# Projections of x and ctx as fp32 products instead of three fp32r passes of split operands

## What is computed

```python
# x: (32, 64, 256), ctx: (32, 64, 128), pos: (32, 64, 2), all fp32
def xattn(x, ctx, pos, Wq, Wkv, Wout, bout):        # 32 heads of 8
    q = (x @ Wq).reshape(b, n, 32, 8)
    k, v = split(ctx @ Wkv, 2)                       # each (b, n, 32, 8)
    q, k = rope(q, pos), rope(k, pos)
    w = softmax(einsum('bqhd,bkhd->bhqk', q, k) / sqrt(8))
    return einsum('bhqk,bkhd->bqhd', w, v).reshape(b, n, 256) @ Wout + bout

x = x + xattn(layernorm(x), ctx, pos, ...)
x = x + soft_moe(layernorm(x), ...)                  # 16 experts of 128 slots, untouched here
```

## Time and profile before

| | |
|---|---|
| device time, median of three runs | 481.79 us (481.67 to 482.77) |
| the profiled execution | 482.33 us, span 480.4 us |
| TensorE busy (matmul) | 445.4 us, 93% of the span |
| VectorE busy | 389.0 us, 81% |
| ScalarE busy | 286.8 us, 60% |
| GpSimd busy | 182.6 us, 38% |
| mean granted TensorE clock | 0.979 of full |

### The profile page before, as it was taken

The page is one execution under the profiler, slowest core; times in us unless marked ns, Lnnn a source line. Parts: engine busy times, 40 slices in busy tenths (PEclk is TensorE's granted clock), DMA queues, the critical chain, the costliest instruction groups (busy, mean ns, idle before and its releaser), DMA issues.

```text
span 480.4 us, 12796 instructions
## 1 busy us (share of the span) xinstructions
PE 445.4 (93%) x4816; PEld 383.2 (80%) x4816; DVE 389.0 (81%) x857; ACT 286.8 (60%) x553; POOL 182.6 (38%) x322
## 2 busy tenths in 40 slices
PE   0679899999999989899999999999999999999995
PEld 0557788778887767778889988988988988988994
DVE  5689788898889985977977977977977887797793
ACT  3357677777888775264465466456457457456532
POOL 4489988469996332114112112112112212202100
PEclk9879799999999999899999999999999999999999
DMA  8930000000002000123223223312312312322321
GB/s 234 279 134 24 2 3 23 1 4 1 1 3 71 3 2 1 41 55 93 57 55 90 57 59 82 75 49 72 82 49 66 93 50 55 98 51 53 94 63 49
DMA packets 27815, 28.54 MB, mean 59 GB/s; under 512 B 10960, under 2 KB 19072, under 8 KB 27520
## 3 DMA queue, kind: packets, MB, share of 16 engines
q1 hardware_dynamic: 27776, 28.00, 22.4%
HBM read 9.11 MB, written 2.10 MB: 23 GB/s over the span
## 4 chain that ended last, share of the span: by engine, by line
PE 68%; DVE 17%; SPq 5%; POOL 4%; DMA 3%; issue 2%; ACT 2%; DVEq 0%; ACTq 0%; POOLq 0%
PE bank L996 12%; PE bank L998 11%; PE bank L997 11%; PE bank L1212 9%; PE bank L1092 6%; PE bank L1230 5%; SPq L293 4%; PE bank L1056 3%; PE bank L1075 3%; PE bank L1113 2%; DVE kT L748 2%; DVE pT L894 2%; DMA xa<-in_x 2%; DVE pb L758 2%; DVE mx L753 2%
## 5 line engine op out<-in xcount | busy, mean ns | idle before, releaser
L894 DVE STREAM_TRANSPOSE pT<-eb 128x512 f32<-128x512 f32 x64 | 44.7, 701 | 37.6 <-ACT eb L618 34.6
L1212 PE MATMUL bank<-w_raw,eb 128*128 128x130 f32 x512 | 62.5, 281 | 0.6 <-DVE w_raw L885 0.6
L1212 PEld LDWEIGHTS bank<-w_raw,eb 128*128 128x128 f32 x512 | 60.2, 195 | 1.9 <-DVE w_raw L885 1.6
L629 ACT ACTIVATE pb<-pb 128x768 f32<-128x768 f32 (+1 forms) x48 | 37.2, 774 | 33.4 <-DVE pb L920 33.4
L624 ACT CAST xlT_h<-bank 128x256 fp32r<-128x256 f32 x16 | 5.9, 371 | 77.6 <-PE bank L1184 77.6
L996 PE MATMUL bank<-mun_h,xlT_l 128*128 128x512 f32 x128 | 52.1, 407 | 0.0
L920 DVE TENSOR_TENSOR pb<-bank,rh 128x384 f32<-128x384 f32 x96 | 49.3, 513 | 3.3
L618 ACT ACTIVATE eb<-bank,nshift,rn 128x512 f32<-128x512 f32 x64 | 46.2, 776 | 7.7 <-PE bank L998 7.6
L998 PE MATMUL bank<-mun_h,xlT_h 128*128 128x512 f32 x128 | 50.5, 395 | 0.0
L997 PE MATMUL bank<-mun_l,xlT_h 128*128 128x512 f32 x128 | 50.5, 394 | 0.0
L545 ACT COPY pT<-bank 128x512 f32<-128x512 f32 x64 | 37.6, 588 | 20.6 <-PE bank L1075 19.7
(11 more groups left out here) (159 smaller groups left out, 1157.1 us busy)
## 6 DMA issues: line engine op xcount, KB each, us to landing
mu_raw<-pT SPq DMA_DIRECT2D x256, 64.0 KB, 2.0
mu_raw<-in_L_ffn_mu SPq DMA_DIRECT2D x1, 2048.0 KB, 10.5
out<-w_raw SPq DMA_DIRECT2D x16, 128.0 KB, 1.9
xa<-in_x SPq DMA_DIRECT2D x1, 1536.0 KB, 8.4
w_raw<-in_L_ffn_W SPq DMA_DIRECT2D x2, 512.0 KB, 9.9
w_raw<-in_L_ffn_W SPq DMA_DIRECT2D x1, 1024.0 KB, 7.8
xa<-in_x SPq DMA_DIRECT2D x1, 512.0 KB, 3.5
ctile<-in_ctx SPq DMA_DIRECT2D x1, 512.0 KB, 5.2
```

The costliest lines, as they stand in the source:

```text
L894: v.transpose(eblk[:, :, 4 * c:4 * c + 4, :].rearrange("p m e j -> p e m j"), eb[:, 4 * c:4 * c + 4, :].rearrange("p e (m j) -> p e m j", ...
L1212: m = mm(bank[HB[i]][:, n * 2 * HC:(n + 1) * 2 * HC], eb[:, e, :], xw[:, e, :], start=True, stop=True)
```

## The change

The split of x, ctx and their weights goes. `wqkv` and `xT` become single fp32 tiles; the weights are loaded straight into their place; ScalarE copies the transposes once, as fp32; each product is one fp32 matmul call. The wait that kept bank 7 in order for `mu_clamp` is now written at `mu_clamp` itself, on ScalarE's copy. The rest of the kernel, and the order of work on every engine, stay.

```diff
-        wqkv = split("wqkv", P, KD + 2, DIM)
+        wqkv = sb("wqkv", P, KD + 2, DIM)
-        xT = split("xT", P, 2, 3, P)
+        xT = sb("xT", P, 2, 3, P)
...
-            sp.dma_start(wqkv_raw[:, 0:KD, :], Wq.rearrange("(k p) n -> p k n", p=P)).then_inc(wqkv_loaded, 16)
-            sp.dma_start(wqkv_raw[:, KD:KD + 2, :], Wkv.rearrange("p (k n) -> p k n", k=2)).then_inc(wqkv_loaded, 16)
+            sp.dma_start(wqkv[:, 0:KD, :], Wq.rearrange("(k p) n -> p k n", p=P)).then_inc(wqkv_loaded, 16)
+            sp.dma_start(wqkv[:, KD:KD + 2, :], Wkv.rearrange("p (k n) -> p k n", k=2)).then_inc(wqkv_loaded, 16)
...
-            act.wait_ge(wqkv_loaded, 32)
-            a.copy(flat(wqkv[0]), flat(wqkv_raw)).then_inc(wqkv_step, 1)
...
-            def xT_high(t):
+            def xT_copy(t):
                 act.wait_ge(xT_filled, t + 1)
-                a.copy(flat(xT[0][:, t % 2]), bank[7][:, 0:3 * P]).then_inc(xT_split, 1)
+                a.copy(flat(xT[:, t % 2]), bank[7][:, 0:3 * P]).then_inc(xT_ready, 1)
...
-            def xT_low(t):
-                dve.wait_ge(xT_split, t + 1)
-                v.tensor_tensor(flat(xT[1][:, t % 2]), bank[7][:, 0:3 * P], flat(xT[0][:, t % 2]).bitcast(F32), ALU.subtract)\
-                    .then_inc(xT_ready, 1)
...
             def mu_clamp(q):
                 dve.wait_ge(muss_ready, q + 1)
+                dve.wait_ge(xT_ready, q + 6)
...
-                if s + 2 < TILES:
-                    xT_low(s + 2)
...
-            dve.wait_ge(wqkv_step, 1)
-            v.tensor_tensor(flat(wqkv[1]), flat(wqkv_raw), flat(wqkv[0]).bitcast(F32), ALU.subtract)\
-                .then_inc(wqkv_ready, 1)
-            xT_low(0)
...
                 for k in range(KD):
-                    mm3(bank[4][:, 0:DIM], [h[:, t % 2, k, :] for h in xT], [h[:, k, :] for h in wqkv],
-                        first=(k == 0), last=(k == KD - 1))
-                mm3(bank[4][:, DIM:2 * DIM], [h[:, t % 2, KD, :] for h in xT], [h[:, KD, :] for h in wqkv])\
+                    mm(bank[4][:, 0:DIM], xT[:, t % 2, k, :], wqkv[:, k, :], start=(k == 0), stop=(k == KD - 1))
+                mm(bank[4][:, DIM:2 * DIM], xT[:, t % 2, KD, :], wqkv[:, KD, :], start=True, stop=True)\
                     .then_inc(qk_filled, 1)
...
-                mm3(bank[6][:, 0:DIM], [h[:, t % 2, KD, :] for h in xT], [h[:, KD + 1, :] for h in wqkv])\
+                mm(bank[6][:, 0:DIM], xT[:, t % 2, KD, :], wqkv[:, KD + 1, :], start=True, stop=True)\
                     .then_inc(v_filled, 1)
...
-            pe.wait_ge(wqkv_ready, 1)
+            pe.wait_ge(wqkv_loaded, 32)
             project_qk(0)
```

More of the change, by code:

```diff
@@ L154, in build @@
         mu_ready = sem("mu_ready")
-        wqkv_step = sem("wqkv_step")
-        wqkv_ready = sem("wqkv_ready")
         shift_step = sem("shift_step")
@@ L166, in build @@
         xT_filled = sem("xT_filled")
-        xT_split = sem("xT_split")
         xT_ready = sem("xT_ready")
@@ L258, in flat @@
             return (t if isinstance(t, bass.AP) else t[:]).rearrange("p a b -> p (a b)")
-        wqkv_raw = flat(pT)[:, 0:(KD + 2) * DIM].rearrange("p (k n) -> p k n", n=DIM)
         w1_raw, w2_raw = w12_raw[:, 0, :], w12_raw[:, 1, :]
@@ L588, in step @@
                 if s + 2 < TILES:
-                    xT_high(s + 2)
+                    xT_copy(s + 2)
                 if s + 1 < TILES:
@@ L649, in _ @@
             act.wait_ge(consts_dve, 3)
-            xT_high(0)
+            xT_copy(0)
             v_copy(0)
-            xT_high(1)
+            xT_copy(1)
             q_copy(0)
@@ L846, in _ @@
             rope_products(0)
-            xT_low(1)
             dve.wait_ge(consts_pool, 4)
```

## The result

The changed kernel takes 485.41 us (median of four runs, 484.96 to 485.93), the kernel before 481.73 beside it (481.53 to 482.77): 3.7 us more, a ratio of 1.0078 [1.0054, 1.0101]. The profiled execution took 485.93 us with a span of 484.1; that of before had 482.33 and 480.4.

The account below looks back on a forecast made before the run. TensorE's queue, closed by one handover to VectorE, was taken to bound the attention steps; +2.54 us there and +0.6 at the start gave +3.1, so 484.9 us against the median 481.79, range 481.9 to 486.4.

Parts of the forecast that it names:

- The bound: Attention steps, 57 to 157 us: TensorE's work end to start, closed by one handover to VectorE; TensorE busy 97.5 of 100.
- The products: Attention projections: project_qk 1.31 to 1.53 us (+0.22), project_v +0.07, priced by project_out; together +2.54 over the steps.
- Four passes: Projections: the skill's count gives 0.48 us a product, project_qk +0.36, project_v +0.12, sum below 4.8; set aside for project_out's 0.43.
- VectorE's saving at nothing: Attention steps: dropping xT_low (0.46 us on the chain) only lengthens the wait before normalise, 0.58 to about 1.2; gain 0.
- no harm from mu_clamp's wait: Steps 3 to 6: mu_clamp waits for ScalarE's copy itself, so the clamp comes earlier, not later; cost 0.
- Rival (c): Steps 2 to 13: VectorE's work sets the period, so each loses 0.46 us, 5.5 in all; 476.3 us, chance 0.07.
- The start: Before the steps from 57 us: tile 1 net +0.18 and project_qk(4) at half clock +0.64; 0.41 to 0.82, taken as 0.6.
- gives 0.46 back: Start, at 28.13 us: without xT_low(2), VectorE's chain up to the variances GpSimd waits for shortens by 0.46 us.
- Rival (a): 50 to 57 us: less TensorE idling removes the half-clock stretch, worth 2.5 us; sum +0.4, 482.2 us, chance 0.15.
- Rival (b): Clock: the same mechanism, its phase moved, adds a half-clock stretch of 2.5 us; 487.4 us, chance 0.09.
- Rival (d): Attention steps: longer products absorbed by TensorE waits the page books as busy; only the ends remain, 481.9 us, chance 0.07.
- The feed-forward part: From 190 us on, TensorE busy 282 of 290 us: untouched by the change and unchanged in length.

Follow-up runs that it names:

- e7: The changed kernel with small fp32 filler matmuls into free PSUM banks where TensorE stood still; 486.35 us, ratio 1.0092.
- e8: The kernel before with small fp32 filler matmuls on TensorE in the same places as e7; 482.95 us, ratio 1.0023.
- e1: The kernel before without VectorE's subtraction xT_low, the high half standing in for the low one, still three passes; 481.90 us, ratio 0.9999.
- e2: The changed kernel with the subtraction put back on VectorE, into a scratch tile; 484.47 us, ratio 1.0068.
- e3: The kernel before with two passes a product instead of three, high x by low weight left out; 477.99 us, ratio 0.9932.
- e10: The kernel before with k's first half transposed into bank 7 and copied ahead of normalise, from tile 1 on; 476.14 us, ratio 0.9861.
- e4: The changed kernel run once more without an edit, for a second trace; 485.77 us, ratio 1.0098.
- e5: The changed kernel with k's first half transposed into bank 6 and copied ahead of normalise, from tile 1 on; 484.04 us, ratio 1.0048.
- e9: The changed kernel with k's first half transposed into bank 7 and copied ahead of normalise, from tile 1 on; 479.90 us, ratio 0.9943.
- e6: The kernel before with k's first half transposed into bank 6 and copied ahead of normalise, from tile 1 on; 481.28 us, ratio 0.9985.

## Why the prediction came out as it did

The forecast was 484.9, or +3.1 us; measured +3.7 between the medians and 3.4 between e7 and e8. Its steps:

- **The bound.** Right. TensorE's queue sets a step's period, closed by one handover to VectorE. e1 (VectorE relieved, 0.9999), e2 (VectorE as before, still 92.78) and e3 (a pass less, 2.9 us less) show it from three sides. What the prediction didn't see is how near the other engines are: in e3 the path over VectorE and ScalarE takes over after 0.2 us in the steps without norm work, and in e10 VectorE's wait is gone.
- **The products.** Right to 0.01: 1.53 for project_qk and 0.43 for project_v on the chain, as taken from project_out. The nine cycles grew by 2.41 (2.45 in e7 and e8) where 2.54 was worked out. The rest is project_v: seven cycles show it, not eight, since step 3's comes ahead of the first k_copy, and with 0.06 instead of 0.07 (9 x 0.22 + 7 x 0.06 = 2.40).
- **Four passes.** By the count of the Trainium skill (FP8 and Floating Point Precision, TensorE Precision Notes), at the trace's 0.12 a pass, an estimate would have been 0.48 a product. The trace of after has 0.43 in two instructions for project_v; the row was the better price.
- **VectorE's saving at nothing, and no harm from mu_clamp's wait.** Right in the steps. The wait before normalise came to 1.06 a step where 1.2 was named. Rival (c) falls with e1.
- **The start.** Too small, and its working wrong. Of the 0.6, +0.18 was to come from tile 1: the longer product +0.64 (measured +0.65 in after against before, 2.90 and 2.25, and +0.59 in e7 against e8) less VectorE's 0.46. The step that failed is "gives 0.46 back": it looked at VectorE alone. GpSimd's list was 0.55 late by the longer product, and VectorE's sum of moments, sped up or not, ended with GpSimd's split. The net was +0.54 instead of +0.18, and 0.82 by tile 2's k_copy, because the later transposes met the half clock. Up to step 3 the change costs 1.07 in e7 against e8, above the upper end of 0.82; with the nine cycles' 2.45 that is 3.5, near what was measured.
- **Rival (a).** Its event came: the half clock of 50 to 57 is gone in the trace of after, and in e4. Its result didn't: other stretches stood at half instead (39 to 46 in one trace, 30 to 37 in the other, where before has 30 to 33), so that no 2.5 us were gained. The prediction priced one stretch as if the others stood still. Rival (b)'s added stretch isn't needed for the result either: e7 and e8 have the difference with none added.
- **Rival (d).** It falls: two of nine cycles absorb a part, and that is project_v's 0.07 alone.
- **The feed-forward part.** "Unchanged in length" failed: 297.60 us from the last normalise but one to the end against 296.18. It wasn't one stray trace. Of the traces without fillers, the five with the change (after, e2, e4, e5, e9) have 296.8 to 297.9 and four of those without it (before, e1, e6, e10) 295.8 to 296.4; but e3, which doesn't have the change either, has 297.8. The six long ones have an issue on SyncE of 1.4 to 1.8 us in the last step, and TensorE's last wait for a DMA is 3.1 to 3.4 us; the four short ones have no such issue there and wait 2.2. The code of this part is the same in all, so the longer products are not the direct cause; that another program ahead of it decides where the long issues fall is likely, and was not tested. The prediction put this part at nothing. In the first pair of traces the total was thus met by a start without loss and a tail with one, which is luck; e7 and e8 show the start's loss, with a tail that has fillers in it.

## What to carry to other kernels

Price a change of precision by an instruction of the same shape in the trace, and ask on which engine the path runs: taking 0.46 us a step from an engine that waits for 0.58 buys nothing, while 0.22 given to the one that sets the period is paid in every step. When an instruction is moved or shortened next to another engine's work, look at what ends together with that work, since a saving ends there. And look for the handover in the cycle rather than for cheaper products: taking k's transpose out of the contested bank was worth 4 us in the same nine cycles.

## What was unexpected of the hardware

The stretches in which TensorE runs at half clock sit elsewhere in two executions of the same kernel (39 to 46 and 476 to 479 in one, 30 to 37 and 166 to 170 in the other), and each moves the steps behind it by one to two us: the k_copy of step 3 lay at 62.50, 64.25 and 64.38 in e2, e4 and after, all with the same products. In the first trace of the kernel after, the granted clock of 20 to 27 is shown as 1.00, while project_qk(1)'s four instructions for q take 2.05 us, 1.10 later on. There the pieces tell the clock, not the column (chain):

```profile
21.27 2.05 PE bank L1001 x4
```

And the long DMA issues on SyncE, such as the one at 469.06 in the kernel after, don't come alone. A transfer of 16 KB on the queue that the page lists for instructions starts at 469.2 (DMA queues from 469 to 470.6: packets, MB, share):

```profile
q8 instruction: 1, 0.02, 3.7%
```

From 190 us on, the thirteen traces have 48 issues of over 0.85 us, and all 48 overlap such a transfer; of the 3488 shorter ones 45 do. That they go together is shown; which of the two waits for the other isn't.
